# Triangle attention on one core: both rows of a step in one PSUM bank, and two d of the last combination multiplied by ScalarE

## The reference, cut to what matters

```
q, k, v1, v2 = (x @ W*).reshape(B, N, N, H, 32)
att = softmax(einsum('bilhd,bljhd->biljh', q, k) / sqrt(32), axis=2)
out = einsum('biljh,bilhd,bljhd->bijhd', att, v1, v2)
```

## Time and profile before

| | us |
|---|---|
| median of 3 runs | 2349.0 (2346.99 to 2353.96) |
| the profiled execution's own time | 2351.3 |
| its span | 2349.5 |
| first step to last copy of a bank | 256 to 1093 |
| MLP's first matmul | 1099.8 |

### The profile page before, as it was taken

One profiled execution on the slowest core, in us unless ns is written; L12 is line 12 of the kernel. 1 busy time (PEld: TensorE's weight loads), 2 busy tenths in 40 slices (PEclk: granted clock), 3 DMA queues, 4 the chain that ended last, 5 costly groups with the idle time before them and its releaser, 6 DMA issues. The chain is left out here.

```text
span 2349.5 us, 43512 instructions
## 1 busy us (share of the span) xinstructions
PE 2033.5 (87%) x17008; PEld 1405.1 (60%) x17008; DVE 2001.5 (85%) x2292; ACT 1303.9 (55%) x2840; POOL 1358.6 (58%) x734
## 2 busy tenths in 40 slices
PE   8989977787788776665999997999999999999997
PEld 7868522232233221111787875888888888888886
DVE  4426799989999999996798885899989999999997
ACT  3337667767766785543232244656565665555553
POOL 1103699989998999996011001455555555666553
PEclk9999999999999999998999998999999999999997
DMA  6768512122321212301134222343222333433432
GB/s 233 249 216 237 145 33 55 42 56 46 66 54 29 38 20 38 94 17 27 54 101 137 81 64 59 68 88 81 74 73 73 90 82 97 108 91 93 105 93 64
DMA packets 300828, 203.98 MB, mean 87 GB/s; under 512 B 202064, under 2 KB 278864, under 8 KB 296528
## 3 DMA queue, kind: packets, MB, share of 16 engines
q1 hardware_dynamic: 282304, 146.51, 25.8%
q0 software_dynamic: 8704, 33.56, 3.9%
q10 hardware_dynamic: 9616, 21.14, 3.1%
HBM read 133.24 MB, written 67.90 MB: 86 GB/s over the span
## 5 line engine op out<-in xcount | busy, mean ns | idle before, releaser
L306 DVE TENSOR_TENSOR att_av<-att_att,att_v2ps 128x2816 f32<-128x2816 f32 (+2 forms) x288 | 775.6, 2753 | 29.4 <-PE att_bank L485 26.5
L306 POOL TENSOR_TENSOR att_av<-att_att,att_v2sb 128x1280 f32<-128x1280 f32 x256 | 744.3, 2933 | 45.6 <-PE att_bank L485 41.5
L485 PE MATMUL att_bank<-att_av,att_w 128*32 128x512 f32 x4096 | 551.0, 617 | 213.0 <-DVE att_av L306 189.8
L485 PEld LDWEIGHTS att_bank<-att_av,att_w 128*32 128x32 f32 x4096 | 138.6, 111 | 563.6 <-issue 282.7
L651 ACT ACTIVATE att_ev<-att_bank 128x512 f32<-128x512 f32 x512 | 296.8, 595 | 262.4 <-PE att_bank L485 218.3
L1864 DVE SCALAR_TENSOR_TENSOR mb_cv<-mb_bank,mb_cw,mb_cv 128x504 f32<-128x504 f32 (+2 forms) x480 | 351.5, 733 | 58.9 <-ACT mb_cv L1658 47.5
L1463 POOL TENSOR_TENSOR mb_y_lo<-mb_y,mb_y_hi 128x1024 fp32r<-128x1024 f32 x60 | 142.5, 2396 | 257.9 <-DVE mb_S L1873 257.9
L1534 PE MATMUL mb_bank<-dt_xT_hi,dt_win_hi 128*128 128x512 f32 x576 | 233.3, 405 | 27.5 <-DVE mb_cv L1864 24.4
L1534 PE MATMUL mb_bank<-dt_xT_lo,dt_win_hi 128*128 128x512 f32 x576 | 226.2, 393 | 0.0
L1534 PE MATMUL mb_bank<-dt_xT_hi,dt_win_lo 128*128 128x512 f32 x576 | 225.9, 392 | 0.0
L1658 ACT ACTIVATE mb_cv<-mb_bank,mb_cw 128x512 f32<-128x512 f32 x160 | 110.0, 690 | 194.6 <-PE mb_bank L1534 193.1
(11 more groups left out here) (199 smaller groups left out, 3864.4 us busy)
## 6 DMA issues: line engine op xcount, KB each, us to landing
att_xin<-in_x SPq DMA_DIRECT2D x32, 512.0 KB, 4.4
qk_t<-att_qk POOLq DMA_DIRECT2D x16, 1024.0 KB, 5.1
v<-att_vs POOLq DMA_DIRECT2D x16, 1024.0 KB, 5.6
mb_dAb<-dA_rows SPq DMA_DIRECT2D x32, 512.0 KB, 6.3
mb_dAb<-dA_cols SPq DMA_DIRECT2D x32, 512.0 KB, 5.7
mixed_t<-att_ev SPq DMA_DIRECT2D x1020, 8.0 KB
att_q<-qk_t ACTq DMA_DIRECT2D x32, 256.0 KB, 4.3
att_kb<-qk_t ACTq DMA_DIRECT2D x64, 128.0 KB, 2.9
```

What stands on the lines that cost most here:

```text
L306: return eng.tensor_tensor(av[t % 2][:, :, d0:d1, :], a.unsqueeze(2).broadcast_to((P, 2, d1 - d0, N)), v2.unsqueeze(1).broadcast_to((P, 2, ...
L485: mm = pe.matmul(bank[r % NB][s * M:(s + 1) * M, :], w[i // WB % 2][:, i % WB, s, :], av[r // 2 % 2][:, i % 2, s * STRIP_D:(s + 1) * STRIP ...
```

## The change

1. Both rows of a step go to **one bank**. The weights get a place for each row (`w` becomes 128 x (4, 2 rows, 4 strips, 32)); for row 0 the columns h2 * 16 + 0 to 7 are filled, for row 1 h2 * 16 + 8 to 15, and the two matmuls of a strip add up in PSUM. The same number of matmuls of the same size runs, but in the order strip 0 row 0, strip 0 row 1, strip 1 row 0, and so on. The three banks now hold three steps. ScalarE makes one copy for a step where it made two, and four builds of 64 x 128 where it made two of 64 x 256. `ev` holds four steps for a buffer; SyncE stores it with 16 DMAs of 8 KB. The order in DRAM stays.
2. At the end of a combination ScalarE turns the three pieces of v2 one behind the other after its copy of step 30; before, it copied row 0 of step 30, turned piece 0, copied row 1 and turned pieces 1 and 2.
3. In the **last combination** (c = 7) ScalarE provides the products of d 30 and 31. It makes them during combination 6, four activations of 128 x 64 in each step, into `q` and `kb`, which are free by then. In the first of these steps it waits for the v2 of the last combination (`v2_loaded`). GpSimd's part ends at d 29; VectorE's takes 21 d in even steps and 20 in odd ones (22 in the first and the last), GpSimd the rest up to d 29. Strip 3 becomes two matmuls of 384 columns and four of 64.
4. The **last store**: SyncE stores the last buffer in two halves (16 DMAs after step 30, then 8 after the last), and ScalarE issues 8 where it issued 4.
5. `rinv` shares the space of `rsum`.

```diff
             def store(c, e):
-                sp.wait_ge(o_copied, c * N + (e + 1) * EB)
-                for d8 in range(STRIP_D // 2 if c * N + (e + 1) * EB == NC * N else STRIP_D):
-                    sp.dma_start(rows.rearrange("(x d) (i j) -> d x i j", d=STRIP_D, i=EB)[d8],
-                                 ev[e % 2][d8:P:16, :, d8 * N:(d8 + 1) * N]).then_inc(o_stored[e % 2], 16)
+                last = c * (N // 2) + (e + 1) * EB == NC * (N // 2)
+                for q0, q1 in ((0, EB // 2), (EB // 2, EB)) if last else ((0, EB),):
+                    sp.wait_ge(o_copied, c * (N // 2) + e * EB + q1)
+                    for d8 in range(STRIP_D // 2 if q1 - q0 < EB and q1 == EB else STRIP_D):
+                        for r in range(2):
+                            sp.dma_start(out_rows(c, e)[d8, r][:, q0:q1],
+                                         ev[e % 2][r * STRIP_D + d8:P:16, q0:q1, d8 * N:(d8 + 1) * N])\
+                                .then_inc(o_stored[e % 2], 16)
...
+        def d_of_dve(t):
+            if t // (N // 2) == NC - 1 and 0 < t % (N // 2) < N // 2 - 1:
+                return DD - 1 - t % 2
+            return DD
...
-            def row(c, i):
-                r = c * N + i
-                need(pe, o_copied, r - NB + 1)
-                for s in range(STRIPS):
-                    if i % 2 == 0 and s == 0:
-                        pe.wait_ge(av_by_dve, r // 2 + 1)
-                    if i % 2 == 0 and s == DD // STRIP_D:
-                        pe.wait_ge(av_by_pool, r // 2 + 1)
-                    mm = pe.matmul(bank[r % NB][s * M:(s + 1) * M, :], w[i // WB % 2][:, i % WB, s, :],
-                                   av[r // 2 % 2][:, i % 2, s * STRIP_D:(s + 1) * STRIP_D, :], start=True, stop=True)
+            def rows(c, step):
+                need(pe, o_copied, t - NB + 1)
+                for s in range(STRIPS):
+                    if s == 0:
+                        pe.wait_ge(av_by_dve, t + 1)
+                    if s == (DD - 2) // STRIP_D:
+                        pe.wait_ge(av_by_pool, t + 1)
+                    n_av = STRIP_D - (NA if s == STRIPS - 1 and c == NC - 1 else 0)
+                    for r in (0, 1):
+                        mm = pe.matmul(bank[t % NB][s * M:(s + 1) * M, 0:n_av * N],
+                                       w[k % 2][:, i0 // 2, r, s, :],
+                                       av[t % 2][:, r, s * STRIP_D:s * STRIP_D + n_av, :], start=(r == 0), stop=(r == 1))
+                    for a in range(STRIP_D - n_av):
+                        for r in (0, 1):
+                            mm = pe.matmul(bank[t % NB][s * M:(s + 1) * M, (n_av + a) * N:(n_av + a + 1) * N],
+                                           w[k % 2][:, i0 // 2, r, s, :],
+                                           by_act[a][:, 2 * step + r, :], start=(r == 0), stop=(r == 1))
...
+            def products(step):
+                if step == 0:
+                    act.wait_ge(scored, PAIRS * NG)
+                    act.wait_ge(v2_loaded, NC * 32)
+                for a in range(NA):
+                    for j in (2 * step, 2 * step + 1):
+                        ins = act.activation(by_act[a][:, :, j], att[(PAIRS - 1) % 2][:, (B - 1) * N:B * N, j], ACT.Copy,
+                                             scale=v2in[:, j, DK - NA + a:DK - NA + a + 1])
...
-                evict(c, 2 * step)
-                if c + 1 < NC and step == N // 2 - 2:
-                    turn_v2(c + 1, 0)
-                evict(c, 2 * step + 1)
+                evict(c, step)
                 if c + 1 < NC and step == N // 2 - 2:
-                    turn_v2(c + 1, 1)
-                    turn_v2(c + 1, 2)
+                    for i in range(NP):
+                        turn_v2(c + 1, i)
...
+                if c == NC - 2:
+                    products(step)
```

More of the change, by code:

```diff
@@ L137, in block_attention @@
     DD = 22
+    DP = 11
+    NA = 2
     M = 32
@@ L157, in block_attention @@
         q = sb("q", [P, N * N])
-        kb = [sb(f"kb{u}", [P, 2, KL, N]) for u in range(2)]
-        least, rsum, rinv = sb("least", [P, N, 2]), sb("rsum", [P, N, 2]), sb("rinv", [P, N, 2])
+        kb_both = sb("kb", [P, 2, 2, KL, N])
+        kb = [kb_both[:, u] for u in range(2)]
+        by_act = [q[:, :].rearrange("p (i j) -> p i j", j=N),
+                  kb_both[:, :, :, :, :].rearrange("p u h (m l) j -> p (u h m l) j", m=1)]
+        least, rsum = sb("least", [P, N, 2]), sb("rsum", [P, N, 2])
+        rinv = rsum
         early = ExitStack()
@@ L180, in block_attention @@
         v1, v2in = [sb(f"v1_{u}", [P, N // 2, DK]) for u in range(2)], sb("v2in", [P, N, DK])
-        v2sb = [sb(f"v2sb{u}", [P, DK - DD, N]) for u in range(2)]
-        w = [sb(f"w{u}", [P, WB, STRIPS, M]) for u in range(2)]
+        v2sb = [sb(f"v2sb{u}", [P, DP, N]) for u in range(2)]
+        w = [sb(f"w{u}", [P, WB // 2, 2, STRIPS, M]) for u in range(2)]
         ident_set, kb_zeroed, q_loaded = sem("ident_set"), sem("kb_zeroed"), sem("q_loaded")
@@ L289, in _ @@
                     load_v2(c + 1)
-                for e in range(N // EB):
+                for e in range(NE):
                     store(c, e)
-                    if c + 1 < NC and e in (7, 14):
-                        sp.wait_ge(w_built, (c * 8 + (4 if e == 7 else 8)) * 2)
-                        load_v1(c + 1, 0 if e == 7 else 1)
+                    if c + 1 < NC and e in (3, 6):
+                        sp.wait_ge(w_built, (c * 8 + (4 if e == 3 else 8)) * 4)
+                        load_v1(c + 1, 0 if e == 3 else 1)
             for u in range(2):
-                sp.wait_ge(o_stored[u], 16 * STRIP_D * (B * PAIRS * N // EB // 2))
+                sp.wait_ge(o_stored[u], STORED * (NC * NE // 2 + u))
             sp.wait_ge(head_loaded, 16 * HEAD)
@@ L434, in _ @@
                 else:
-                    product(dve, t, v2d, 0, DD).then_inc(av_by_dve, 1)
+                    product(dve, t, v2d[:, 0:d_of_dve(t)], 0, d_of_dve(t)).then_inc(av_by_dve, 1)
                 if n < PAIRS and m in LEAST_AT:
@@ L550, in _ @@
                         pe.wait_ge(v_by[e], 2 * XN)
-                for i in (0, 1):
-                    row(t // (N // 2), t % (N // 2) * 2 + i)
+                rows(t // (N // 2), t % (N // 2))
                 if n < PAIRS:
@@ L638, in build, with evict @@
                     act.wait_ge(v1_loaded[half], c * 32 + 32)
-                need(act, i_done, (c * 8 + k - 1) * WB)
+                need(act, i_done, (c * 8 + k - 1) * WB // 2)
                 for h2 in range(2):
                     r = slice(h2 * N, (h2 + 1) * N)
-                    act.activation(w[k % 2][r, :, :, h2 * 16:h2 * 16 + STRIP_D],
-                                   v1[half][r, (k % 4) * WB:(k % 4 + 1) * WB, :]
-                                   .rearrange("p i (s d) -> p i s d", s=STRIPS), ACT.Copy).then_inc(w_built, 1)
-            def evict(c, i):
-                e = i // EB
-                if i % EB == 0:
-                    need(act, o_stored[e % 2], (c * (N // EB // 2) + e // 2) * 16 * STRIP_D)
-                act.wait_ge(i_done, c * N + i + 1)
-                act.activation(ev[e % 2][:, i % EB, :], bank[(c * N + i) % NB][:, :], ACT.Copy).then_inc(o_copied, 1)
-                if i % WB == 1 and i // WB < 7:
-                    build(c, i // WB + 1)
-                if c + 1 < NC and i == N - 7:
+                    v = v1[half][r, (k % 4) * WB:(k % 4 + 1) * WB, :].rearrange("p (q i) (s d) -> p q i s d", i=2, s=STRIPS)
+                    for i in range(2):
+                        to = h2 * 16 + i * STRIP_D
+                        act.activation(w[k % 2][r, :, i, :, to:to + STRIP_D], v[:, :, i], ACT.Copy).then_inc(w_built, 1)
+            def evict(c, step):
+                t, e = c * (N // 2) + step, step // EB
+                if step % EB == 0:
+                    need(act, o_stored[e % 2], (c * (NE // 2) + e // 2) * STORED)
+                act.wait_ge(i_done, t + 1)
+                act.activation(ev[e % 2][:, step % EB, :], bank[t % NB][:, :], ACT.Copy).then_inc(o_copied, 1)
+                k = step * 2 // WB
+                if step * 2 % WB == 0 and k < 7:
+                    build(c, k + 1)
+                if step * 2 % WB == 0 and k == 7 and c + 1 < NC:
                     build(c + 1, 0)
```

45 lines of the change are left out of this document (31 added, 14 removed).

## The result

The changed kernel takes 2360.0 us (median of 8 runs, 2357.01 to 2363.04), the kernel before 2349.6 in the same session. The ratio is 1.0042 [1.0032, 1.0052], so the change costs some 10 us. The profiled execution took 2357.3 us with a span of 2355.5, 6.0 more than the span before.

What follows compares the result with a forecast made beforehand. VectorE was taken as the bound, GpSimd close behind. The terms -9 + 0 + 2.4 + 5 - 5 + 9 = +2.4 us, laid on the median of 2349.0, gave 2351.4, with a range of 2335 to 2366.

Steps and rivals of the forecast that it cites:

- rival 3: Whole kernel: the two ends cost their full price, little is won back; +16 us, near 2365, chance 0.22.
- the turns of v2: Combination boundaries: piece 0 comes later, VectorE waits net 0.6 us at four of them; +2.4 us, ends 0 and +5.
- the last store: Stage end: the MLP waits for SyncE's 24 issues, 12.7 us after the last copy; +9, ends +3 and +10.
- One bank for a step: VectorE's idle time: more banks and store buffer steps remove most of 15 us of waits; -9, ends 0 and -15.
- The prediction's own rule: First 11 steps of a pair: scores stand between rows, so TensorE has no room; VectorE waits 0.71 us per two steps.
- The order of the matmuls: TensorE's queue: two rows of a strip behind each other leave a step's sixteen matmul records at 1.92 us; 0.
- Rival 2: TensorE's queue in every step: strips go one by one; +85, about +200 or about +600 us, together chance 0.17.
- The reason given against it: Earlier trace of a steady step: four matmul records run within 0.64 us from 955.03, each over 0.59 long.
- ScalarE's wait for v2: Start of combination 6: v2's load queues behind 16 store issues, VectorE starts late; +5 us, ends +2 and +9.
- The last combination: Combination 7: VectorE's thirty steps lose 45 d, -6.0 us; with two bounds rubbing -5, ends -6 and -2.
- Rivals 1 and 4: Waits vanish wholly, issues cheap: near 2335, chance 0.15; last combination keeps 3.0 us a step: +5, no separate chance.

Runs made afterwards that it cites:

- e9: Changed kernel with piece 0 of v2 turned before the copy of step 30, last buffer stored whole, no products of ScalarE: 2345.1 us, ratio 0.9981.
- e3: Changed kernel without the products of ScalarE, GpSimd multiplying all its d in the last combination too: 2362.2 us, ratio 1.0045.
- e5: Changed kernel with the matmuls row by row again (rows outside, strips inside), still in one bank: 2359.6 us, ratio 1.0039.
- e7: Changed kernel with each matmul cut in two halves of 256 columns, eight records of a strip in a row: 2683.6 us, ratio 1.1412.
- e6: Changed kernel with piece 0 of v2 turned ahead of the copy of step 30: 2354.6 us, ratio 1.0015.
- e1: Changed kernel with the last v2 loaded ahead of the last store of combination 5: 2353.5 us, ratio 1.0014.
- e11: Same kernel as e8 (changed kernel with three repairs), run again in a later session: 2338.0 us, ratio 0.9944.
- e4: The changed kernel itself run again, unedited, as baseline: 2362.5 us, ratio 1.0045.
- e8: Changed kernel with last v2 loaded one store earlier, last buffer stored whole, piece 0 turned before the copy of step 30: 2335.8 us, ratio 0.9934.
- e10: Changed kernel with the half matmuls of e7, but strips taking turns between the halves, four records in a row: 2363.3 us, ratio 1.0051.

## Why the prediction was off by some 9 us

The direction was left open (+2.4 us, 0.46 for no measurable change); the result, +10.5 in the medians, lies above that, in the range and inside rival 3. In the profiled executions the sum is +6.0 where +2.4 was forecast. Two terms were short, the turns of v2 and the last store, and one was too small a gain, the bank. Term by term:

**One bank for a step, -9.** Of the waits it named, those for stores went: ScalarE's fell from 42.3 us in 16 waits to 2.2 in one, and the waits of 3.61 and 2.16 us of the earlier trace rows have no successor of that cause. Sixteen issues for four steps made no later store wait for long. Alone, in e9, the bank brings 14.6, close to the end of -15, but with shorter turns and a higher clock in it, so it is not shown that the banks and buffers are worth that much. The waits in pairs of steps with scores stay, at 0.76. In the kernel before, the two waits of the earlier trace rows stand beside stretches of lower clock too (the window from 916.4 to 920 had a granted clock of 0.50), which the term did not ask about.

**The turns of v2, +2.4, ends 0 and +5: the term furthest off.** The visible wait came out as worked out, 5.3 us where it was 2.8, +2.5. But the late piece 0 cost 10.5 us in all (e3 against e9), since the term priced VectorE's wait and put at nothing what the same delay does to TensorE. Product by product, e3 falls behind e9 by 5.0 us at the turns to combinations 2, 4, 6 and 7 (1.35, 1.37, 1.36 and 0.94) and by 7.2 more behind them. This second part comes in ten pieces of 0.2 to 0.9 us. Six follow at once on a stretch in which e3 had the lower clock and e9 had not, and the other four (0.66 to 0.70) come two or nine steps behind one. Where e9 was the one with such a stretch, in combinations 0 and 3, it lost 0.65 to 0.90 at a time in the same way, 3.2 us in all, while e3 lost 1.2 in combination 1; so 2 us of the 12.2 come back. The prediction's own rule that TensorE has no room in the first 11 steps of a pair does not explain it: at the full clock the delay does not grow in them (468 to 512 in the changed kernel). That the longer idle time of TensorE brings the lower clock is shown for the turns (19 of 21 against none of 15). Further on in the two combinations TensorE's idle time was 2.17 to 2.18 us with either order. There it is only seen that all seven executions with the late piece had one or two more such stretches in combinations 2 and 4 each, and those with the early piece none in combination 2 and none or one in 4. Why is open. No term of the prediction asks for the clock.

The two errors nearly cancel: -14.6 + 10.5 = -4.1 is what e3 shows against the kernel before, where -9 + 2.4 = -6.6 was forecast.

**The order of the matmuls, 0.** Right: 1.95 us for 1.92, and e5 shows that it is free. Rival 2 did not come true, but its mechanism exists: e7 pays 324 us over the changed kernel. The reason given against it, shows only that two waiting records pass. It could not tell that three do; that the edge lies above four records and not at them was luck as far as the trace of before goes.

**ScalarE's wait for v2, +5.** The mechanism was right to the place: the load behind sixteen stores, ScalarE queued behind it, VectorE at the end. The size was 6.4. Counted from the first store behind the last copy of combination 5 (892.90), VectorE was out of work at 16.9 (916.14 less 6.37), where 15.5 was worked out, and started again at 23.2 instead of 20.2. Of these 3.0 us the load brings 1.7: sixteen stores took 10.3 us instead of 9.7 and a load 1.55 to issue where 0.6 was taken, so that it landed at 17.7 instead of 16. The four activations bring 0.3, at 0.407 and 0.410 us instead of 0.339. The last us is, by what is left, TensorE's: after 6.5 us of idle time its two steps of 32 records took 6.3 us, since the granted clock was 0.57, for a part of them the lower level of 1.2 GHz. The row of that window in the changed kernel (columns as in e6):

```profile
912.40:918.70 6.30, 6.29 (x32) 1.66 (x32) 2.56 (x1) 6.25 (x21) 2.51 (x1) 0.57 0.03 7
```

**The last combination, -5.** Right: from GpSimd's first product to the last copy 100.1 us became 94.7, -5.4, and against e3 it is -6.2, the lower end. VectorE's forms took 2947 and 2815 ns, within 0.01 us of one d at 0.133; strip 3's short records did no harm.

**The last store, +9.** The choice of the price was right and the sum short: +11.3. Buffer 6's issues ended 0.7 us ahead of the last copy and not 1.8, and the issues took 0.644 us, not 0.605, which is 0.9 over 24 of them. The lower end of +3 rested on a DMA of half the size being cheaper, and it is not.

**What is left.** The spans of the two profiled executions are 6.0 apart, the medians 10.5. The difference lies in the third column of the table, which no run touches: 1248.0 to 1255.7 us. It is the clock. The window of the first 10 us of the MLP (columns as in e6), in the changed kernel and then in e1:

```profile
1105.90:1115.90 10.00, 5.22 (x16) 4.03 (x16) 3.44 (x12) 1.58 (x2) 3.62 (x5) 0.84 0.34 84
```

```profile
1102.20:1112.20 10.00, 6.58 (x16) 4.92 (x16) 3.17 (x10) 0.64 (x1) 3.59 (x4) 0.67 0.19 33
```

The same sixteen matmuls run at a granted clock of 0.84 in one and 0.67 in the other. Summed from the MLP's first matmul to the end, the time that the trace records at the lower level goes with the column through all thirteen executions of the table: 53 us in e11 (1248.0), 58 in before, changed and e5 (1249.6 to 1249.7), 66 in e4 and e8 (1253.4 and 1253.7), 70 to 71 in the others (1254.5 to 1255.7). The eight executions of the changed kernel show the same in whole: 2357.0 to 2357.9 us at a mean granted clock of 0.974 to 0.975, 2359.6 to 2363.0 at 0.971 to 0.973. The profiled one was among the fast ones. Whether a longer idle time of TensorE ahead of the MLP (in the changed kernel the MLP starts 17.8 us behind the last copy, before it was 6.5) makes the slower course more frequent was not tried; e8 and e11, one kernel, show both courses.

**The chances.** Rival 3 (0.22), "the two ends cost their full price and little is won back", came true in its numbers: it set -3 for the bank with its turns at +4 and 8 and 10 for the two ends. The two ends did cost 6.4 and 11.3. The bank was not weak, though: what it brought was given back at the turns. Rivals 1 and 4 fell: the issues are not cheap, and the last combination runs at 2.8 us a step (TensorE's steps between 1040 and 1052 start 2.73 to 2.86 apart).

## What to carry to other kernels

Where a step is moved behind another on an engine, price not only the wait that it makes but the idle time that it gives to TensorE behind it, and look at the granted clock of the steps that follow: here 1.4 us more of idle time at a turn was followed by a step of 16 records in 3.56 us instead of 1.95. When two executions of one kernel differ, compare the granted clock stretch by stretch before blaming an edit. Count DMA issues behind the last event and not their bytes: two halves of a transfer cost twice its issue time (0.567 us each), and an early half helps only if the queue is free to take it. And when three costs of a good change are each a line or two in the order of a queue (load before store, piece before copy, whole before halves), repairing them may be worth more than the change itself: here 24 us of repairs, a part of them a higher clock, turned a loss of 10 us into a gain of 12 to 16.

## What the runs showed of the hardware

- A column strip of TensorE takes up to four matmul records behind each other (one running, three waiting) without holding up the other strips: 1.95 to 1.97 us a step. With eight it holds them up: over 4 us (e7 against e10). What lies between (five to seven) is open.
- The issue of a small DMA on SyncE's queue took 0.567 us and the next began 0.605 to 0.65 later than it, the same for the halved transfers as for the whole ones.
- Where TensorE stood idle for 2.37 to 2.44 us at a turn in the middle of a busy stage, its granted clock fell to the lower level within a microsecond in 19 of 21 cases; after 1.02 to 1.07 us it fell in none of 15, after 1.84 in none of 3. In between the outcome differs from execution to execution: after an idle time of 2.17 us the window from 514.9 to 518.9 of the changed kernel ran at 0.57, after 2.18 the same step of e6 took its 1.95 us at 1.00.
- Time at the lower level moved the part of the program behind the attention, with no edit in it, from 1248.0 us (53 us of it at the lower level) to 1255.7 (71).
